# Two layers of a decoder on one core: fewer score pieces in the Top-64 stages, three probability buffers and an earlier turn of the maxima in the dense cross attention

## The chip, the core and the metric

One core of a Trainium2 chip runs the whole program. Its engines are TensorE (PE, matrix products into PSUM), VectorE (DVE), ScalarE (ACT), GpSimd (POOL) and SyncE (SP, which issues DMA transfers here). They run side by side, each through its own instruction list in order, and are held together by semaphores. The metric is the time of one execution on the device in microseconds (us).

## The reference, cut to what matters

Two decoder layers over 2,048 tokens of width 256 with a context of 1,601 tokens. The two stages with Top-64 have 16 heads of width 16:

```
# layer 0, cross attention: 2048 queries, 1601 keys, 16 heads
vals, idx = jax.lax.top_k(scores, 64)
scores = full_like(scores, neg).at[..., idx].set(vals)
ctx = softmax(scores) @ vh
# layer 1, self attention: 2048 queries, 2048 keys, 16 heads
top_scores, top_idx = jax.lax.top_k(scores, 64)
out = softmax(top_scores) @ gathered v
# layer 1, dense cross attention: 2048 queries, 1601 keys, 16 heads of width 64
attn = softmax(einsum('bqhd,bkhd->bhqk', q * SCALE, k))
out = einsum('bhqk,bkhd->bqhd', attn, v)
```

Around them stand a causal attention, a mixture of experts, a last linear layer and the norms.

## The kernel before

**Order of the stages.** `decoder` calls them one after the other, with a barrier between: load, `l0ac` (causal), `l0xc` (`attend_top`, 1,601 keys), experts, `l1ac` (`attend_top`, 2,048 keys), the wide projections, `l1xc` (`attend_wide`), `finish_wide`, the last linear layer. Within a stage each engine has a list of its own, written out by hand, and `hold` puts the semaphore waits before a step.

**`attend_top`.** A tile is 128 queries of one head against all keys, so a stage has 16 x 16 = 256 tiles. For tile n:
- PE forms the scores in 4 chunks (`search`, L557) into two PSUM banks, and ACT copies them to one of 4 score buffers (L652, tiles `l0xc_score` or `l1ac_score` and `keep_xT`). ACT may do so when `checked` and `masked` say that the tile four before is finished with the buffer.
- DVE cuts the row in `NSEG` = 64 pieces, all `nk // 64` wide but for the last. `MAX8` takes the 8 largest of each piece (L745) to `cand`, ordered so that the largest of all pieces come first, then the second largest, and so on.
- In the next tile's time DVE draws the 64 largest from `cand` in 8 rounds, each a `MAX8` (L764, `tops`) and, but for the last, a match-and-replace (L766). Round r reads only the first `UPTO[r]` candidates, `NSEG` times 1, 1, 1, 2, 2, 3, 4, 8. Between two steps of this chain stand pieces of the new tile (`some_segments`), so the chain's own waits are covered.
- ACT counts how many scores are above and below the 64th value found (`count`, L658 and L662), PE sums this over the queries (`flag`, L602) and ACT stores it (L667, `anyflag`). Late in the tile after the next DVE reads it (`check`, L780). If it isn't zero, DVE draws the 64 largest from the whole row again (L790 and L792, 15 steps) and writes the mask anew (L797, L799): the fallback. It counts up `checked` (L802).
- POOL writes the mask of the scores below the 64th value (L527). PE adds it to the transposed scores (`unit`, L571 and L573), ACT takes the exponential (`weigh`, L680), PE forms the weighted sums (L585), and after each chunk of 4 tiles it turns them (`combine`, L596).

**`attend_wide`.** For each head the keys stand in 13 tiles (`NKT`), 12 of 128 and one of 65. PE computes scores transposed, key by query, in key tile j (`by_key`: L1926 adds the shift by the row maximum, L1930 the product); ACT takes the exponential of 4 chunks of 512 queries to the probability buffer `prob[buf(j)]` (L2015); PE forms the sums of the key tile before (`sums`, L1942); POOL stages a value tile (L1888) and adds the probabilities of all key tiles to `total` (L1878, and L1875 for tiles 0 and 1 in one step), from which PE forms the denominators (L1952). `freed(h, j)` is the number of additions that ACT waits for before it writes the buffer of tile j.

Beside head `hb` runs the search for the row maxima of the next head `ha`: 64 jobs (16 query tiles, 4 key chunks), which `jobs_of(j)` spreads over the key tiles. A job is two matmuls on PE (`by_query`, L1915 and L1916) into one of 3 banks and a reduction on DVE (L2057). After the last of them DVE counts up `stats_set` (`a_set`), PE turns the 16 columns of maxima (`a_end`, L1987), DVE splits them in two parts (`a_split`), and SP sends them by 8 small DMAs (L1843) to the row `shift`, which PE needs for key tile 0 of the next head.

```
def buf(j):
    return 2 if j == NKT - 1 else j % 2
def freed(h, j):
    if j >= 2 and j < NKT - 1:
        return added_after(h, j - 2)
    return ADDS * (h - 1) + {0: NKT - 3, 1: NKT - 2, NKT - 1: NKT - 1}[j] + ADDS
```

## Time and profile before

| | us |
|---|---|
| median of 3 runs (9,355.04 to 9,376.61) | 9,370.65 |
| the profiled execution, own time | 9,320.69 |
| its span in the trace | 9,318.9 |
| DVE busy | 6,784.5 (73%) |
| PE busy | 6,964.9 (75%) |
| ACT busy | 4,490.9 (48%) |
| POOL busy | 3,923.4 (42%) |

The shares are means over stages with different limits, so each stage has to be read by itself: first the slices of the page, then the busy times of its stretch, then the order of the instructions in one tile. Busy times of overlapping instructions are counted once. A row of the timeline has the start, the time to the end of the last of its instructions, the engine, the line, the operation with its tiles and the count; in brackets stands the idle time before it and what ended it.

### The profile page before, as it was taken

Reading aid. Unit: us, or ns where it says so; the run is one execution under the profiler, and the core shown is the slowest. Engines: PE = TensorE matmul, PEld = TensorE weight load, DVE = VectorE, ACT = ScalarE, POOL = GpSimd, SP = SyncE. Lnnn points to the kernel's source line nnn. Section 1 sums busy time; section 2 is a strip of 40 time slices with the busy share of each in tenths; the row PEclk is TensorE's granted clock in tenths of the full one; section 3 lists DMA queues with packets and bytes.
Section 4 is the critical chain, followed back from the end, with each engine's and each line's share of the span. In section 5 each row is a group of like instructions: output and inputs, shape, how many; then the busy total and the mean of one; then the engine's idle time right before and its main releaser. Section 6 shows DMA issues by size and latency. Waiting matters only on the chain. (4 is left out here: it accounts for less than half of the span.)

```text
span 9318.9 us, 164285 instructions
## 1 busy us (share of the span) xinstructions
PE 6964.9 (75%) x31345; PEld 2804.8 (30%) x31468; DVE 6784.5 (73%) x47597; ACT 4490.9 (48%) x8515; POOL 3923.4 (42%) x2595
## 2 busy tenths in 40 slices
PE   6998667666666656999666666666656899999983
PEld 2333222222222224555222222222223322222212
DVE  2764599999999993554699999999997344344423
ACT  1564466666666652111476776677655322222220
POOL 0000255454545541221365656556553055555550
PEclk7998666666666665999666776766767999999986
DMA  2000000000000000000000000000000411111113
GB/s 62 26 21 5 34 5 8 5 8 5 8 6 7 8 1 16 14 20 10 35 5 8 5 8 5 8 5 8 5 5 9 161 30 29 29 40 32 29 30 73
DMA packets 81598, 193.31 MB, mean 21 GB/s; under 512 B 23728, under 2 KB 38062, under 8 KB 77230
## 3 DMA queue, kind: packets, MB, share of 16 engines
q1 hardware_dynamic: 72366, 169.98, 6.5%
q10 hardware_dynamic: 8192, 12.59, 0.5%
q14 instruction: 769, 6.30, 0.2%
q8 instruction: 271, 4.44, 0.2%
HBM read 118.97 MB, written 62.76 MB: 20 GB/s over the span
## 5 line engine op out<-in xcount | busy, mean ns | idle before, releaser
L2057 DVE TENSOR_REDUCE l1xc_part_max<-l1xc_by_query 128x1 f32<-128x512 f32 (+1 forms) x1024 | 558.0, 571 | 865.3 <-PE l1xc_by_query L1916 772.7
L557 PE MATMUL l1ac_by_query<-l1ac_k_stack,l1ac_q_stack 97*128 (+1 forms) x1024 | 441.5, 497 | 790.8 <-ACT keep_xT L652 436.3
L2015 ACT ACTIVATE l1xc_prob<-l1xc_less_max 128x512 f32<-128x512 f32 (+1 forms) x832 | 451.3, 594 | 1118.7 <-PE l1xc_less_max L1930 973.7
L745 DVE MAX8 l1ac_cand<-l1ac_score 128x8 f32<-128x32 f32 x8192 | 956.3, 185 | 27.9 <-ACT l1ac_score L652 16.9
L745 DVE MAX8 l1ac_cand<-keep_xT 128x8 f32<-128x32 f32 x8192 | 953.4, 183 | 4.4
L557 PE MATMUL l0xc_by_query<-l0xc_k_stack,l0xc_q_stack 97*128 (+2 forms) x1024 | 387.9, 448 | 724.2 <-ACT keep_xT L652 505.4
L745 DVE MAX8 l0xc_cand<-l0xc_score 128x8 f32<-128x25 f32 (+1 forms) x8192 | 896.0, 177 | 33.6 <-ACT l0xc_score L652 15.8
L745 DVE MAX8 l0xc_cand<-keep_xT 128x8 f32<-128x25 f32 (+1 forms) x8192 | 897.4, 177 | 4.4
L527 POOL TENSOR_SCALAR l1ac_lost<-l1ac_score,l1ac_tops 128x2048 bf16<-128x2048 f32 x128 | 695.8, 5436 | 472.8 <-DVE l1ac_tops L764 472.8
L1878 POOL TENSOR_TENSOR l1xc_total<-l1xc_total,l1xc_prob 128x2048 f32<-128x2048 f32 (+1 forms) x176 | 793.8, 4510 | 71.5 <-POOL l1xc_v_tile L1888 71.2
L527 POOL TENSOR_SCALAR l1ac_lost<-keep_xT,l1ac_tops 128x2048 bf16<-128x2048 f32 x128 | 696.1, 5438 | 271.6 <-DVE l1ac_tops L764 271.6
L527 POOL TENSOR_SCALAR l0xc_lost<-l0xc_score,l0xc_tops 128x1601 bf16<-128x1601 f32 x128 | 554.8, 4334 | 514.3 <-DVE l0xc_tops L764 509.2
L527 POOL TENSOR_SCALAR l0xc_lost<-keep_xT,l0xc_tops 128x1601 bf16<-128x1601 f32 x128 | 554.7, 4333 | 310.5 <-DVE l0xc_tops L764 310.5
L764 DVE MAX8 l1ac_tops<-l1ac_cand 128x8 f32<-128x64 f32 (+4 forms) x2048 | 669.6, 327 | 0.3
L764 DVE MAX8 l0xc_tops<-l0xc_cand 128x8 f32<-128x64 f32 (+4 forms) x2048 | 669.4, 327 | 0.4
L680 ACT ACTIVATE l1ac_prob<-l1ac_less_max 128x512 f32<-128x512 f32 x1024 | 583.5, 590 | 109.8 <-PE l1ac_less_max L573 103.0
L571 PE MATMUL l1ac_less_max<-l1ac_far,l1ac_lost 128*128 128x128 bf16 x4096 | 561.4, 282 | 4.2 <-POOL l1ac_lost L527 4.2
L680 ACT ACTIVATE l0xc_prob<-l0xc_less_max 128x512 f32<-128x512 f32 (+1 forms) x832 | 483.0, 592 | 154.7 <-PE l0xc_less_max L573 153.7
L573 PE MATMUL l1ac_less_max<-l1ac_q_stack,l1ac_k_stack 100*128 (+1 forms) x1024 | 550.4, 537 | 0.0
L571 PEld LDWEIGHTS l1ac_less_max<-l1ac_far,l1ac_lost 128*128 128x128 bf16 x4096 | 390.6, 129 | 528.2 <-issue 507.3
L1309 DVE TENSOR_REDUCE l0ac_part_max<-l0ac_by_query 128x1 f32<-128x512 f32 (+3 forms) x640 | 366.9, 608 | 196.3 <-PE l0ac_by_query L1173 85.9
L1930 PE MATMUL l1xc_less_max<-l1xc_q,l1xc_k 64*128 64x512 f32 (+1 forms) x1664 | 499.3, 678 | 0.0
(455 smaller groups left out, 14631.2 us busy)
## 6 DMA issues: line engine op xcount, KB each, us to landing
l1xc_k<-wide_k SPq DMA_DIRECT2D x32, 400.2 KB, 5.2
moe_w<-in_L_ffn_mlp_w_dram SPq DMA_DIRECT2D x16, 512.0 KB, 4.2
wide_q<-l1xp_full SPq DMA_DIRECT2D x8, 1024.0 KB, 3.9
wide_q_parts<-l1xp_parts SPq DMA_DIRECT2D x16, 512.0 KB, 5.3
l1xc_q_hm<-wide_q_parts SPq DMA_DIRECT2D x32, 256.0 KB, 3.8
l1xc_q<-wide_q SPq DMA_DIRECT2D x32, 256.0 KB, 5.7
wide_sums<-l1xc_o_out ACTq DMA_DIRECT2D x64, 128.0 KB, 2.3
l1xf_num<-wide_sums SPq DMA_DIRECT2D x16, 512.0 KB, 11.7
```

What stands on the lines that cost most here:

```text
L527: nc.gpsimd.tensor_scalar(lost[:, i % 8, 0:nk], score[i % 4][:, 0:nk], tops[:, i % 8, TOPK - 1:TOPK], None, ALU.is_lt).then_inc(masked, 1)
L557: nc.tensor.matmul(sA[c % 2][:, 0:w], Qm[0:SHIFT_ROW, bass.ds(at + i * P, P)], Kb[0:SHIFT_ROW, bass.ds(at + a, w)], start=True, stop=True) ...
L571: nc.tensor.matmul(bank[0:w, t * P:(t + 1) * P], lost[:, (4 * c + t) % 8, j * P:j * P + w], far[:], start=(t == 0), stop=False, skip_group ...
L573: nc.tensor.matmul(bank[0:w], Kb[:, bass.ds(at + j * P, w)], Qm[:, bass.ds(at + c * CH, CH)], start=False, stop=True, skip_group_check=Tru ...
L680: nc.scalar.activation(prob[0:w, k % 2, j % 4], yP[y_bank(c, j)][0:w], ACT.Exp).then_inc(y_taken, 1)
L745: seg = nc.vector.max(new[:, j:8 * NSEG:NSEG], score[i % 4][:, a:a + w])
L764: ins = nc.vector.max(some, part)
L1309: nc.vector.tensor_reduce(part_max[:, i % 2, c:c + 1], sA[k % 3][:, 0:seen_keys(i, c)], AX.X, ALU.max).then_inc(a_taken, 1)
L1878: nc.gpsimd.tensor_tensor(total[0:n], total[0:n], prob[0:n, buf(j)], ALU.add).then_inc(added_p, 1)
L1930: nc.tensor.matmul(yP[r][0:n], k32[half, key], q32[half, at], start=False, stop=True).then_inc(y_formed, 1)
L2015: nc.scalar.activation(prob[0:n, buf(j), c], yP[c % 2][0:n], ACT.Exp).then_inc(y_taken, 1)
L2057: nc.vector.tensor_reduce(part_max[:, i % 2, c:c + 1], a_bank(i, c)[:, 0:w], AX.X, ALU.max).then_inc(a_taken, 1)
```

## The change

It has two parts. In `attend_top` the row is cut in 52 pieces in place of 64. Their edges are rounded evenly, so the pieces have 30 or 31 columns with 1,601 keys and 39 or 40 with 2,048. `cand` and the prefixes `UPTO` follow `NSEG`. In `attend_wide` the probability and value buffers go round in three (tile 12 takes buffer 1), `freed` follows, the 64 jobs are spread over the first 11 key tiles (tiles 0 to 8 have 6, tiles 9 and 10 have 5; before, tiles 0 to 3 had 6 and tiles 4 to 11 had 5), and `a_set`, `a_end` and `a_split` stand one key tile earlier.

```
-    NSEG = 64
-    seg_w = nk // NSEG
-    segs = [(j * seg_w, seg_w if j < NSEG - 1 else nk - j * seg_w) for j in range(NSEG)]
+    NSEG = 52
+    edges = [(2 * j * nk + NSEG) // (2 * NSEG) for j in range(NSEG + 1)]
+    segs = [(edges[j], edges[j + 1] - edges[j]) for j in range(NSEG)]
...
-            return 2 if j == NKT - 1 else j % 2
+            return 1 if j == NKT - 1 else j % 3
...
-            early = len(jobs) - 5 * (NKT - 1)
+            early = len(jobs) - 5 * (NKT - 2)
             start = 5 * j + min(j, early)
-            return jobs[start:start + 5 + (1 if j < early else 0)] if j < NKT - 1 else []
+            return jobs[start:start + 5 + (1 if j < early else 0)] if j < NKT - 2 else []
...
-            if j >= 2 and j < NKT - 1:
-                return added_after(h, j - 2)
-            return ADDS * (h - 1) + {0: NKT - 3, 1: NKT - 2, NKT - 1: NKT - 1}[j] + ADDS
+            if j == NKT - 1:
+                return added_after(h, NKT - 3)
+            if j >= 3:
+                return added_after(h, j - 3)
+            return added_after(h - 1, (NKT - 4, NKT - 1, NKT - 2)[j])
...
-                    if j == NKT - 1 and ha is not None:
+                    if j == NKT - 2 and ha is not None:
                         a_end(ha)
...
+                    if j == NKT - 3 and ha is not None:
+                        a_set(ha)
                     if j == NKT - 2 and ha is not None:
-                        a_set(ha)
-                    if j == NKT - 1 and ha is not None:
                         a_split(ha)
```

DVE at the start of a tile of l0xc, before: pieces (`cand<-keep_xT`) between the steps of the chain.

```order
L764 MAX l0xc_tops<-l0xc_cand 128x8
L745 MAX l0xc_cand<-keep_xT 128x8 x4
L766 MATCH_REPLACE l0xc_cand<-l0xc_tops,l0xc_cand 128x64
L745 MAX l0xc_cand<-keep_xT 128x8 x4
L764 MAX l0xc_tops<-l0xc_cand 128x8
L745 MAX l0xc_cand<-keep_xT 128x8 x4
L766 MATCH_REPLACE l0xc_cand<-l0xc_tops,l0xc_cand 128x64
L745 MAX l0xc_cand<-keep_xT 128x8 x3
L764 MAX l0xc_tops<-l0xc_cand 128x8
L745 MAX l0xc_cand<-keep_xT 128x8 x4
```

The same place in the change:

```order
L764 MAX l0xc_tops<-l0xc_cand 128x8
L745 MAX l0xc_cand<-keep_xT 128x8 x3
L766 MATCH_REPLACE l0xc_cand<-l0xc_tops,l0xc_cand 128x52
L745 MAX l0xc_cand<-keep_xT 128x8 x3
L764 MAX l0xc_tops<-l0xc_cand 128x8
L745 MAX l0xc_cand<-keep_xT 128x8 x3
L766 MATCH_REPLACE l0xc_cand<-l0xc_tops,l0xc_cand 128x52
L745 MAX l0xc_cand<-keep_xT 128x8 x3
L764 MAX l0xc_tops<-l0xc_cand 128x8
L745 MAX l0xc_cand<-keep_xT 128x8 x3
```

Three pieces stand between the steps in place of 3 or 4, and the replaced prefix has 52 candidates in place of 64.

PE at the end of a head of l1xc, before (L1987 is the turn of the maxima, L1942 sums, L1926 and L1930 the scores of a key tile; 65 rows are key tile 12):

```order
L1915 MATMUL l1xc_by_query<-l1xc_k_hh,l1xc_q_hm 128x65
L1916 MATMUL l1xc_by_query<-l1xc_k_m,l1xc_q_hm 128x65
L1942 MATMUL l1xc_o_sum<-l1xc_prob,l1xc_v_tile 64x512 x2
L1987 MATMUL l1xc_den<-keep_ident,l1xc_stat 16x128
L1777 ISA
L1926 MATMUL l1xc_less_max<-l1xc_shift,l1xc_onesb 65x512 x2
L1930 MATMUL l1xc_less_max<-l1xc_q,l1xc_k 65x512 x2
L1942 MATMUL l1xc_o_sum<-l1xc_prob,l1xc_v_tile 64x512 x2
L1777 REGISTER_ALU
L1926 MATMUL l1xc_less_max<-l1xc_shift,l1xc_onesb 65x512 x2
L1930 MATMUL l1xc_less_max<-l1xc_q,l1xc_k 65x512 x2
L1942 MATMUL l1xc_o_sum<-l1xc_prob,l1xc_v_tile 64x512 x2
```

The same place in the change, where the lines are two further down:

```order
L1944 MATMUL l1xc_o_sum<-l1xc_prob,l1xc_v_tile 64x512 x2
L1989 MATMUL l1xc_den<-keep_ident,l1xc_stat 16x128
L1777 ISA
L1928 MATMUL l1xc_less_max<-l1xc_shift,l1xc_onesb 128x512 x2
L1932 MATMUL l1xc_less_max<-l1xc_q,l1xc_k 128x512 x2
L1944 MATMUL l1xc_o_sum<-l1xc_prob,l1xc_v_tile 64x512 x2
L1777 REGISTER_ALU
L1928 MATMUL l1xc_less_max<-l1xc_shift,l1xc_onesb 128x512 x2
L1932 MATMUL l1xc_less_max<-l1xc_q,l1xc_k 128x512 x2
L1944 MATMUL l1xc_o_sum<-l1xc_prob,l1xc_v_tile 64x512 x2
L1777 ISA
L1928 MATMUL l1xc_less_max<-l1xc_shift,l1xc_onesb 65x512 x2
```

The turn now stands before key tile 11 (128 rows), and key tiles 11 and 12 follow it without jobs of the search.

## Rows read from the trace of the kernel before

**Rows 1.** The page, busy tenths of DVE in 40 slices of the span.

```profile
...
DVE  2764599999999993554699999999997344344423
...
```

**Rows 2.** Busy time in three stretches (l0xc, l1ac, l1xc); columns in the first line.

```profile
...
core 0: us, PE busy (x) PEld busy (x) DVE busy (x) ACT busy (x) POOL busy (x), PEclk, DMA share, GB/s
1060.00:3520.00 2460.00, 1638.20 (x7782) 644.81 (x7783) 2424.36 (x21958) 1488.61 (x3038) 1221.55 (x882) 0.61 0.02 6
4540.00:7110.00 2570.00, 1702.78 (x9093) 687.19 (x9092) 2547.79 (x21950) 1755.06 (x3217) 1502.22 (x883) 0.69 0.02 6
7400.00:9061.00 1661.00, 1510.60 (x6245) 395.45 (x6352) 655.07 (x1327) 469.98 (x865) 914.64 (x398) 0.94 0.14 31
...
```

**Rows 3.** Timeline of DVE in an l0xc tile (start, us, instructions), and a page row.

```profile
...
2042.86 0.67 DVE L764 MAX8 l0xc_tops<-l0xc_cand 128x8 f32<-128x512 f32 x1
2043.45 0.77 DVE L745 MAX8 l0xc_cand<-keep_xT 128x8 f32<-128x25 f32 x8
...
L745 DVE MAX8 l0xc_cand<-l0xc_score 128x8 f32<-128x25 f32 (+1 forms) x8192 | 896.0, 177 | 33.6 <-ACT l0xc_score L652 15.8
...
```

**Rows 4.** Timeline of DVE, first and next instruction of the fallback in l0xc and l1ac.

```profile
...
3350.72 1.83 DVE L790 MAX8 l0xc_top_full<-keep_xT 128x8 f32<-128x1601 f32 x1
...
3382.62 0.09 DVE L766 MATCH_VALUE_LOAD l0xc_cand<-l0xc_tops,l0xc_cand 128x8 f32 x1 [0.61 <-DVE l0xc_lost L799]
...
6782.69 2.28 DVE L790 MAX8 l1ac_top_full<-l1ac_score 128x8 f32<-128x2048 f32 x1
...
6821.97 0.09 DVE L766 MATCH_VALUE_LOAD l1ac_cand<-l1ac_tops,l1ac_cand 128x8 f32 x1 [0.33 <-DVE l1ac_lost L799]
...
```

**Rows 5.** Waits in the l0xc stretch: total us, times, longest.

```profile
...
ACT keep_xT L652 <- DVEq L802: 441.8, 126, 33.7
...
```

**Rows 6.** Timeline of ACT in l0xc, and two loads of the flag (line 780).

```profile
...
2023.30 1.09 ACT L652 ACTIVATE keep_xT<-l0xc_by_query 128x512 f32<-128x512 f32 x2 [3.41 <-DVEq L802]
...
2033.34 1.08 ACT L652 ACTIVATE l0xc_score<-l0xc_by_query 128x512 f32<-128x512 f32 x2
...
2038.82 0.16 ACT L667 ACTIVATE l0xc_anyflag<-l0xc_turned 1x1 f32<-1x1 f32 x1
...
L780 DVEq TENSOR_LOAD <-l0xc_anyflag x1: 305/305/305, 2022.6 to 2022.6; - x1
...
L780 DVEq TENSOR_LOAD <-l0xc_anyflag x1: 304/304/304, 2041.4 to 2041.4; - x1
...
```

**Rows 7.** Waits in the l1xc stretch: total us, times, longest.

```profile
...
ACT l1xc_prob L2015 <- POOL l1xc_total L1875: 103.6, 16, 6.6
...
```

**Rows 8.** Timeline of PE in one head of l1xc, rows of line 1926.

```profile
...
7853.32 0.39 PE L1926 MATMUL l1xc_less_max<-l1xc_shift,l1xc_onesb 2*128 2x512 bf16 x2 [3.35 <-DMA l1xc_shift<-l1xc_stat_parts]
...
7858.81 0.39 PE L1926 MATMUL l1xc_less_max<-l1xc_shift,l1xc_onesb 2*128 2x512 bf16 x2
...
7863.33 0.39 PE L1926 MATMUL l1xc_less_max<-l1xc_shift,l1xc_onesb 2*128 2x512 bf16 x2
...
7866.86 0.39 PE L1926 MATMUL l1xc_less_max<-l1xc_shift,l1xc_onesb 2*128 2x512 bf16 x2
...
7870.38 0.39 PE L1926 MATMUL l1xc_less_max<-l1xc_shift,l1xc_onesb 2*128 2x512 bf16 x2
...
7877.14 0.39 PE L1926 MATMUL l1xc_less_max<-l1xc_shift,l1xc_onesb 2*128 2x512 bf16 x2 [2.76 <-ACT l1xc_prob L2015]
...
7882.25 0.39 PE L1926 MATMUL l1xc_less_max<-l1xc_shift,l1xc_onesb 2*128 2x512 bf16 x2
...
7944.44 0.40 PE L1926 MATMUL l1xc_less_max<-l1xc_shift,l1xc_onesb 2*65 2x512 bf16 x2
...
7952.83 0.40 PE L1926 MATMUL l1xc_less_max<-l1xc_shift,l1xc_onesb 2*128 2x512 bf16 x2 [3.40 <-DMA l1xc_shift<-l1xc_stat_parts]
...
```

**Rows 9.** Busy time and granted clock of short stretches of l1xc, columns as rows 2.

```profile
...
7952.90:7956.40 3.50, 3.17 (x8) 0.97 (x10) 0.04 (x1) 1.08 (x2) 1.99 (x1) 0.53 0.56 135
...
8052.70:8072.00 19.30, 19.08 (x51) 4.07 (x54) 3.84 (x7) 4.31 (x8) 2.29 (x2) 0.50 0.58 130
...
```

## The prediction

> **What bounds the kernel now.** I read the page's slices first, then the busy times of three stretches, then the order of instructions inside one tile of each. [rows 1] VectorE (DVE) shows 9s in two long blocks, slices 6 to 15 and 21 to 30. They are the two Top-64 stages, l0xc (1,601 keys) and l1ac (2,048 keys). [rows 2] In them DVE is busy 2,424 of 2,460 us and 2,548 of 2,570 us, while TensorE (PE) has about two thirds and ScalarE (ACT) 60 to 68%. So DVE sets their time, and every nanosecond that it drops is worth one, until a neighbour becomes late. The third row of [rows 2] is the dense cross attention l1xc: PE 1,511 of 1,661 us, nothing else above 914. It is bound by PE, and a gain there is either idle time of PE or a higher clock.
>
> [rows 6] One l0xc tile per 9.40 us: the two value loads stand two tiles apart, 2022.6 and 2041.4. A tile has 64 `MAX8` over pieces (25 columns) and a chain of 8 `MAX8` and 7 match-and-replace over the candidates.
>
> **Part 1, fewer pieces.** What a `MAX8` costs DVE is the distance to the next start, not its duration, since they overlap: eight pieces take 0.77 us from the first start to the last end, one lasts 0.177, so the other seven are (0.77 - 0.177)/7 = 0.085 us apart [rows 3]. The one over 512 candidates blocks for 2043.45 - 2042.86 = 0.59 us. Two points give a line: 0.085 = f + 25s, 0.59 = f + 512s, so s = 1.04 ns a column and f = 59 ns an instruction. The columns of a row stay (1,601 or 2,048), so 12 pieces less save 12 x 59 = 0.71 us a tile. The chain reads 1+1+1+2+2+3+4+8 = 22 piece counts in its `MAX8` and 14 in its replacements: 36 x 12 = 432 columns less, 0.45 us. Together 1.16 us a tile: 9.40 to 8.24 in l0xc, and in l1ac, with 447 columns more, 9.87 to 8.71. For 2 x 256 tiles: **-594 us**. Between two chain steps now 3 pieces stand in place of 3 or 4, some 0.27 us against 0.21 us for the shortest step with its own 0.13 already behind it, so the chain's waits stay covered.
>
> Priced by duration (0.177 us for 25 columns, so some 0.15 fixed) the 12 pieces would be worth 1.8 us a tile. The Trainium skill says something near that ("VectorE: DVE Perf Modes", section on the TRN2 errata): its table has 58 cycles fixed, but it finds about 150 measured for a single operation and calls this an overhead that many small tiles pay each time. By the 150 the 12 pieces save 1.9 us; by the trace's distances 0.7. Two neighbours overlap here, so I keep 0.7.
>
> **What the wider pieces bring back.** Each piece gives only its 8 largest. If 9 of a row's 64 lie in one piece (or the short prefixes of the first rounds take a wrong value) the count misses, and `check` does the whole row again. This is a matter of the data, so I worked it out from the reference: its scores for the drawn inputs, in float32, cut both ways. With 64 pieces no row of l0xc fails and one of l1ac (head 14, tile 0); with 52 pieces 4 rows of l0xc in 4 tiles and 4 of l1ac in 4 tiles, each with 9 in one piece. The trace has one fallback in each stage [rows 4], so l0xc has one that the cut does not explain; I take it for two equal scores at the cut, which comes again. So 4 more in l0xc and 3 more in l1ac. [rows 4] One costs 3382.62 - 3350.72 = 31.9 us in l0xc and 6821.97 - 6782.69 = 39.3 in l1ac, and DVE does nothing else: 4 x 31.9 + 3 x 39.3 = **+246 us**. PE, ACT and GpSimd (POOL) only drain meanwhile.
>
> **Who is late next.** DVE waits for ACT at two places: the scores of the next tile, and the flag before `check`. [rows 5] ACT itself waits 441.8 us in 126 turns for `checked` on one pair of score buffers, so it has slack of 2 to 3 us a tile that shrinks by 1.16. The scores come most of a tile early. The flag is nearer. [rows 6] The ACT slot that ends a chunk (every fourth) runs from 2023.30 to 2033.34, 10.04 us, longer than a tile already; the next begins 1.3 us after a check (2022.6 + 9.4) and its flag is out 5.6 us later, at 2038.98, 2.4 us before the load at 2041.4. With 8.24 us a tile the slow slot starts 0.7 us after its check and ends 10.74 - 8.24 = 2.5 us after the next one; 2.5 + 5.6 is 8.1 us against 8.24, and a slot that is 0.6 us slower in its matmuls (an estimate) makes it 8.7. DVE then waits up to 0.5 us at 64 such places: 0 to 32 us. I take **+30**, since the granted clock there is 0.61 in the mean, nearer to half than to full [rows 2]. l1ac has 0.47 us more in each tile for the same slot, and I take none. POOL's mask keeps below a tile in both.
>
> **Part 2, the dense cross attention.** Three things move.
> (a) *Three probability buffers.* Before, key tile 2 shared its buffer with tile 0, and the first addition (4.5 us on POOL) reads 0 and 1 together. ACT waits for it in each of 16 heads, 103.6 us [rows 7]. On PE the tile takes 7882.25 - 7870.38 = 11.87 us against 7.05 for tile 1, with as many matmuls [rows 8]: 2.76 us idle, the rest slower matmuls behind it. After, tile 2 has its own buffer and tile 3 finds the addition done. Tile 12 now takes buffer 1, and the next head's tile 1 waits for its addition, which ends some 5 us into tile 0; it is needed after about 8. Gain 4.8 us a head.
> (b) *Maxima turned at the last but one key tile.* The transpose stands right before 7944.44, the shifts land at 7952.83, and PE is idle 3.40 us at the head's border [rows 8]. A tile earlier the same 8.6 us lie under two tiles without scores, about 10.3 us. Gain 3.4 us. SP's queue is not held up: its K and Q loads follow these DMAs and are for the next head.
> (c) *The score jobs* of tile 11 go to tiles 4 to 8, one more each. The same matmuls, so nothing in sum; DVE takes six reductions in a tile elsewhere already. Without them POOL (5.2 us a tile) is close behind PE for two tiles; 0 to 0.5 us a head.
> *The clock.* After such an idle stretch PE runs at half: granted clock 0.53 from 7952.90 [rows 9], the 1.2 GHz level. That doubles the first part of key tile 0: 7858.81 - 7853.32 = 5.49 us against 3.53 at tile 1 [rows 8], 1.96 us more. Together (a), (b) and the clock are 10.2 us for each of 15 borders, 152; behind some borders the half clock lasts longer (0.50 over 19.3 us, second row), which I price at 20 for all of them. Lower end: only the idle time, 2.8 + 3.4 in 15 heads, 93. Upper end 180. I take **-165**, near the upper end, since rows show the clock lost right behind the idle stretch. The Trainium skill agrees in kind ("TensorE: Matmul & The Clock Gate", "Why this matters for your kernels"): idle gaps between bursts of matmuls bring the half rate back.
>
> **The sum.** -594 + 246 + 30 - 165 = -483 us against the profiled run's own 9,320.7 us (span 9,318.9). The median of the shown runs is 50 us higher, 9,370.65; the difference carries over: **8,888 us**.
>
> **The rivals.**
> - *The wait for the flag takes the place of the pieces.* If ACT and PE cannot follow, DVE idles before `check` and about half of part 1 stays away. For it: the 10.04 us slot. Against it: that slot is one in four and ACT idles behind the others. +297: 9,185.
> - *The wait in l1xc only moves.* Additions on POOL or the DMA of the shifts become late at another tile, and the clock keeps falling. Only some 30 of 165 us come: 9,023.
> - *Slower: the fallbacks multiply.* The chip's scores are sums of split parts, not my float32. Without fallbacks the change is worth 594 - 30 + 165 = 729 us, and one costs 35.6 on average: above 20 more fallbacks it loses. With 30 more, 9,710. Against it: a miss is decided by which piece a score stands in, and my rows with 9 are decided far above rounding; the cut before gave the counts that the trace has, but for one.
> - *Pieces priced by duration.* If a piece frees its whole fixed 0.15 us, part 1 gives 600 us more: 8,290. Against it are the distances in [rows 3]. The rule of the Trainium skill above would make this time.
> - *It does not do what it says*: the fallbacks stay at two, since the misses of 52 pieces do not occur on the chip: 8,888 - 246 = 8,642.
>
> **How the numbers follow.** My case 0.74, flag 0.08, moved wait in l1xc 0.10, slower 0.03, priced by duration 0.02, no more fallbacks 0.03. Own range of my case: two fallbacks fewer or two more (72), the flag 0 to 60, l1xc -93 to -180, runs that differ by 20: 8,800 to 8,990. To hold 8 in 10 it takes in the near side of the moved wait: 8,800 to 9,010. A measurement of this kernel can tell about 0.2% (19 us) from no change. All cases but one are faster by more: faster 0.96, same 0.01, slower 0.03.
>
> **What would show it.** In the profile after: value loads 8.24 and 8.71 us apart, with 52 pieces between; long `MAX8` rows (1,601 columns) in 5 tiles and (2,048) in 4; DVE still in the 9s of both blocks. An idle time of DVE before the load of the flag would speak for the first rival. In l1xc: no wait of ACT for POOL at key tile 2, no wait of PE for the shift DMA, key tiles 0 and 2 near 8.1 and 7.1 us, a granted clock near 1.0 throughout, the stretch near 1,495 us. I am wrong if the number of fallbacks is not near nine, or if the tiles do not shorten by the fixed cost of 12 pieces.

## The result, and the profile after

| | before | after |
|---|---|---|
| median, us (4 runs each, on one chip) | 9,362.85 | 8,966.16 |
| lowest to highest | 9,352.21 to 9,376.61 | 8,950.63 to 8,971.08 |
| the profiled execution, own time | 9,320.69 | 8,971.08 |

The ratio is 0.9583, with a 95% interval from 0.9558 to 0.9607: the change takes 397 us off, where 483 were forecast (8,888, range 8,800 to 9,010). The sign, the two waits that went and the number of fallbacks came as predicted. 86 us of the gain stayed away, about half in each part of the change; a new wait of PE for ACT, which the prediction did not have, and idle time of DVE that it put too low are behind most of it.

The busy times of the three stretches in the profile after, columns in the first line; they answer to [rows 2]:

```profile
core 0: us, PE busy (x) PEld busy (x) DVE busy (x) ACT busy (x) POOL busy (x), PEclk, DMA share, GB/s
1060.00:3400.00 2340.00, 1538.75 (x7784) 615.84 (x7785) 2266.07 (x19009) 1471.44 (x3041) 1224.99 (x883) 0.65 0.02 6
4420.00:6840.00 2420.00, 1620.57 (x9069) 657.88 (x9068) 2371.56 (x18952) 1741.65 (x3218) 1499.19 (x882) 0.72 0.02 6
7165.00:8712.00 1547.00, 1469.45 (x6350) 383.46 (x6348) 659.39 (x1328) 469.95 (x865) 914.37 (x398) 0.98 0.15 34
```

DVE still fills the two Top-64 stages, with about 3,000 instructions fewer in each, but it now stands idle for 74 us in l0xc and 48 in l1ac, against 36 and 22 in [rows 2]. PE's granted clock in l1xc rose from 0.94 to 0.98.

The same chain steps as in [rows 3] and the order rows of the change, DVE in l0xc after:

```profile
2054.38 0.30 DVE L764 MAX8 l0xc_tops<-l0xc_cand 128x8 f32<-128x156 f32 x1
2054.60 0.36 DVE L745 MAX8 l0xc_cand<-l0xc_score 128x8 f32<-128x31 f32 x3
2054.88 0.07 DVE L766 MATCH_VALUE_LOAD l0xc_cand<-l0xc_tops,l0xc_cand 128x8 f32 x1
```

Three pieces of 31 columns take 2054.88 - 2054.60 = 0.28 us from start to start, 0.093 each, and 156 candidates take 2054.60 - 2054.38 = 0.22. The line of the prediction gives 0.091 and 0.221.

The fallback's `MAX8` over a whole row (line 790, eight in each fallback) after; [rows 4] had one fallback a stage:

```profile
L790 DVE MAX8 l1ac_top_full<-l1ac_score x32: 2294/2295/2295, 4765.4 to 6653.8; 128x8 f32<-128x2048 f32 x32
L790 DVE MAX8 l0xc_top_full<-l0xc_score x24: 1827/1828/1830, 1126.4 to 2241.7; 128x8 f32<-128x1601 f32 x24
L790 DVE MAX8 l0xc_top_full<-keep_xT x16: 1828/1828/1830, 2297.4 to 3270.8; 128x8 f32<-128x1601 f32 x16
```

(24 + 16)/8 = 5 fallbacks in l0xc and 32/8 = 4 in l1ac, the nine that were forecast.

By stage, from the first to the last instruction in the two traces:

| us | before | after | difference |
|---|---|---|---|
| l0xc | 2,515.3 | 2,388.1 | -127.2 |
| l1ac | 2,626.7 | 2,479.5 | -147.2 |
| l1xc | 1,671.5 | 1,556.8 | -114.7 |
| all others | 2,505.4 | 2,544.9 | +39.5 |

The three stages give -389, 8 us short of what the medians show. Of the 39 us outside them 25.6 lie in l1af, the 16 output rows behind l1ac, whose code is the same. The profiled execution of before was 42 us quicker than its median, and its short l1af may be one reason; that is not shown. Two windows of 10 us at the same place in that stage, one of the run with attend_wide alone changed (l1af 36.0 us, as before) and one of after (61.6 us):

```profile
7129.00:7139.00 10.00, 10.00 (x44) 6.09 (x44) 2.46 (x6) 1.19 (x2) 0.00 (x0) 1.00 0.01 2
```

```profile
6890.00:6900.00 10.00, 10.00 (x23) 5.56 (x23) 1.27 (x3) 0.60 (x1) 0.00 (x0) 0.50 0.00 0
```

PE is busy throughout in both, with 44 matmuls at a granted clock of 1.00 (2.4 GHz) and 23 at 0.50 (1.2 GHz). Over all profiles of this study the stage took 36.0, 40.4 or 61.6 us, so a difference of 26 us there says nothing of a change.

### The profile page after: what moved, and what is told of

Its sections match the earlier page's. It is cut to its first block and busy times, and to the rows that moved or that the text cites. A ratio compares the mean times of both kernels' runs of the same rounds, so it can differ in the third digit from the quotient of the medians.

```text
span 8969.3 us, 158459 instructions
## 1 busy us (share of the span) xinstructions
PE 6782.5 (76%) x31468; PEld 2754.4 (31%) x31468; DVE 6449.7 (72%) x41621; ACT 4457.7 (50%) x8515; POOL 3925.8 (44%) x2595
## 5 line engine op out<-in xcount | busy, mean ns | idle before, releaser
L745 DVE MAX8 l1ac_cand<-l1ac_score 128x8 f32<-128x39 f32 (+1 forms) x6656 | 863.8, 193 | 28.7 <-ACT l1ac_score L652 16.8
L745 DVE MAX8 l1ac_cand<-keep_xT 128x8 f32<-128x39 f32 (+1 forms) x6656 | 863.7, 192 | 4.4
L745 DVE MAX8 l0xc_cand<-l0xc_score 128x8 f32<-128x31 f32 (+1 forms) x6656 | 801.9, 183 | 28.0 <-ACT l0xc_score L652 15.7
L745 DVE MAX8 l0xc_cand<-keep_xT 128x8 f32<-128x31 f32 (+1 forms) x6656 | 802.3, 182 | 4.4
L764 DVE MAX8 l1ac_tops<-l1ac_cand 128x8 f32<-128x52 f32 (+4 forms) x2048 | 598.6, 292 | 0.3
L764 DVE MAX8 l0xc_tops<-l0xc_cand 128x8 f32<-128x52 f32 (+4 forms) x2048 | 597.7, 292 | 0.3
L571 PE MATMUL l1ac_less_max<-l1ac_far,l1ac_lost 128*128 128x128 bf16 x4096 | 532.2, 270 | 7.7 <-POOL l1ac_lost L527 4.5
L573 PE MATMUL l1ac_less_max<-l1ac_q_stack,l1ac_k_stack 100*128 (+1 forms) x1024 | 527.0, 515 | 0.0
L571 PEld LDWEIGHTS l1ac_less_max<-l1ac_far,l1ac_lost 128*128 128x128 bf16 x4096 | 366.8, 122 | 491.4 <-issue 422.1
L1932 PE MATMUL l1xc_less_max<-l1xc_q,l1xc_k 64*128 64x512 f32 (+1 forms) x1664 | 474.7, 647 | 0.0
```

Source lines behind the costliest of these rows:

```text
L571: nc.tensor.matmul(bank[0:w, t * P:(t + 1) * P], lost[:, (4 * c + t) % 8, j * P:j * P + w], far[:], start=(t == 0), stop=False, skip_group ...
L573: nc.tensor.matmul(bank[0:w], Kb[:, bass.ds(at + j * P, w)], Qm[:, bass.ds(at + c * CH, CH)], start=False, stop=True, skip_group_check=Tru ...
L745: seg = nc.vector.max(new[:, j:8 * NSEG:NSEG], score[i % 4][:, a:a + w])
L764: ins = nc.vector.max(some, part)
L1932: nc.tensor.matmul(yP[r][0:n], k32[half, key], q32[half, at], start=False, stop=True).then_inc(y_formed, 1)
```

## The experiments

All were timed in five rounds beside the kernel before, in groups of four on one chip: e1 to e4, then e5, e6, e7 and e9, then e8, e11, e12 and e13 (before: 9,352, 9,364 and 9,346 us). A difference of medians between two groups carries the difference of these three numbers; the stages in the traces do not.

| run | median us | ratio to before, 95% interval |
|---|---|---|
| the change | 8,966 | 0.9583 [0.9558, 0.9607] |
| e1 pieces only | 9,092 | 0.9733 [0.9700, 0.9766] |
| e2 attend_wide only | 9,221 | 0.9875 [0.9842, 0.9908] |
| e3 three buffers only | 9,306 | 0.9961 [0.9941, 0.9981] |
| e4 earlier turn only | 9,275 | 0.9910 [0.9876, 0.9943] |
| e5 change, no second search | 8,616 | 0.9205 [0.9177, 0.9234] |
| e6 change, store spread | 8,906 | 0.9510 [0.9481, 0.9539] |
| e7 change, 51 and 53 pieces | 8,780 | 0.9366 [0.9336, 0.9396] |
| e8 e6 and e7 | 8,726 | 0.9330 [0.9297, 0.9364] |
| e9 change, combine late | 8,936 | 0.9534 [0.9504, 0.9564] |
| e11 e9 and flag early | 8,901 | 0.9520 [0.9483, 0.9556] |
| e12 e6, e7 and e11 | 8,685 | 0.9286 [0.9259, 0.9313] |
| e13 40 pieces, no second search | 8,419 | 0.9004 [0.8970, 0.9038] |

### The parts apart

e1 is the change with attend_wide as before.

> The change's part in attend_top alone (52 pieces with even edges), attend_wide as before. The prediction's terms give -594 for shorter tiles, +246 for 7 more fallbacks and +30 for the flag wait: -318 against before. The two traces (before and the whole change) show -127 in l0xc and -147 in l1ac: -274, with 8.30 us for a tile of l0xc and 8.72 of l1ac, 5 and 4 tiles of over 30 us, and the flag wait in one tile of four of l0xc. If what the trace shows is the parts' own and they don't touch each other: -274, near 9,089 us. If the stretch after l1ac (finish_rows, 36 to 62 us) belongs to this part, -249. A rival: some of the gain seen in the stages came from the heads of attend_wide through the clock; then less than 240 of it is here.

e2 is the kernel before with the changed attend_wide.

> The change's part in attend_wide alone, attend_top as before. The prediction had -165 for it; the traces show the PE stretch of l1xc going from 1,660.4 to 1,546.0, -114. Parts that add up: near 9,249 us (-114), and the sum of this run's and e1_pieces_only's differences is within 15 us of the whole change's -397. A rival: the stretch of l1xc has luck of the clock in it (two heads of the profiled run had 20 us at half clock); then this run's l1xc is nearer 1,500 and the time -150.

Measured: 0.9733 and 0.9875. The two gains add up, 0.0267 + 0.0125 = 0.0392 against 0.0417 of the whole change, within the intervals. In the traces e1's l0xc and l1ac are 2,388.3 and 2,478.3 us long, the whole change's to about 1 us, with 5 and 4 fallbacks; e2's l1xc is 1,550.5. So the parts don't touch each other, and each is worth less than its forecast: by the medians 260 us (318 forecast) and 132 (165). l1af was 61.6 us in e1 and 36.0 in e2.

### Two edits inside attend_wide

e3 has the buffers alone:

```
-            return 2 if j == NKT - 1 else j % 2
+            return 1 if j == NKT - 1 else j % 3
...
+            if j >= 3:
+                return added_after(h, j - 3)
```

> Before, with only the three buffers in turn (buf and freed) in attend_wide; the jobs and the turn of the maxima stay where they were. The wait of ACT for POOL at key tile 2 (103.6 us over 16) goes: key tile 2 of a head from 11.87 to 7.4, 15 times 4.45 = -67. Theory A, from the trace of the whole change: ACT's 8 DMA issues of store then lie in front of the exponentials of key tile 3, which becomes 1.5 us longer: +24; the wait for the shift row stays (3.4 a head, at times more). Sum -43, near 9,320. Rival B: the new wait at key tile 3 comes from the sixth job there and from the earlier turn, not from the store; then no wait is at key tile 3 here and the gain is -67 (9,296).

e4 has the jobs, `a_end`, `a_set` and `a_split` alone:

```
-            early = len(jobs) - 5 * (NKT - 1)
+            early = len(jobs) - 5 * (NKT - 2)
...
-                    if j == NKT - 1 and ha is not None:
+                    if j == NKT - 2 and ha is not None:
                         a_end(ha)
```

> Before, with only the earlier turn in attend_wide (64 jobs over 11 key tiles, a_set, a_end and a_split one key tile earlier); the buffers stay as they were. The wait for the shift row ahead of key tile 0 goes: 15 times 3.4 = -51, and the half clock behind it (about 2 us a head): -80 at most, near 9,285 to 9,312. Key tile 2 keeps its wait of 4.5 us for POOL, and since ACT is held there the store's issues cost nothing at key tile 3. With e3_buffers_only it should add up to e2_wide_only. Rival: the two idle times stand in for each other (PE's idle 4.5 us at key tile 2 throws the clock to half again, whatever comes at key tile 0); then this part alone gives under 40.

Measured: -46 us and -77 us (ratios 0.9961 and 0.9910), together -123 against -132 for both. Waits in the l1xc stretch. Before, beside the wait for POOL of [rows 7], ACT had this one (total us, times, longest):

```profile
ACT l1xc_prob L2015 <- issue: 41.3, 9, 5.0
```

Of e3:

```profile
ACT l1xc_prob L2017 <- issue: 73.3, 15, 5.6
PE l1xc_less_max L1928 <- DMA l1xc_shift<-l1xc_stat_parts: 57.4, 16, 7.8
```

and of e4:

```profile
ACT l1xc_prob L2015 <- POOL l1xc_total L1875: 103.7, 16, 6.6
PE l1xc_less_max L1926 <- DMA l1xc_shift<-l1xc_stat_parts: 7.8, 1, 7.8
```

Each edit removes the wait that it is aimed at and leaves the other one. e3 has lost the wait for POOL of [rows 7], but its ACT now stands 73.3 us at 15 places for "issue", that is for nothing that another engine owes it, where before had 41.3 at 9. Key tile 2 went from 11.85 to 7.45 us in e3 and key tile 3 from 7.56 to 8.72 (medians over heads 1 to 14 of 0 to 15), and PE stands 24.2 us for ACT inside tile 3 in place of 6.4. Theory A holds: the wait came with the buffers alone, without the earlier turn. e4 has the shift DMA only once, at the first head.

### What stands ahead of key tile 3

Where the 67.3 us of "issue" of the whole change lie, ACT in one head after (ACTq is ACT's queue, which issues a DMA):

```profile
7701.40 0.59 ACT L2017 ACTIVATE l1xc_prob<-l1xc_less_max 128x512 f32<-128x512 f32 x1
7701.94 0.81 ACTq L2034 DMA_DIRECT2D wide_sums<-l1xc_o_out  x1
7702.91 0.48 ACTq L2032 DMA_DIRECT2D wide_sums<-l1xc_o_out  x1
...
7706.10 0.48 ACTq L2034 DMA_DIRECT2D wide_sums<-l1xc_o_out  x1
7706.85 1.09 ACT L2017 ACTIVATE l1xc_prob<-l1xc_less_max 128x512 f32<-128x512 f32 x2 [4.85 <-issue]
```

and PE in the same head, line 1928 being the first matmul of a group:

```profile
7702.96 0.39 PE L1928 MATMUL l1xc_less_max<-l1xc_shift,l1xc_onesb 2*128 2x512 bf16 x2
7707.99 0.39 PE L1928 MATMUL l1xc_less_max<-l1xc_shift,l1xc_onesb 2*128 2x512 bf16 x2 [1.44 <-ACT l1xc_prob L2017]
7713.10 0.39 PE L1928 MATMUL l1xc_less_max<-l1xc_shift,l1xc_onesb 2*128 2x512 bf16 x2
```

Six of the eight issues of `store` stand from 7702.91 to 7706.10 at (7706.10 - 7702.91)/5 = 0.64 us each, and ACT's exponentials are behind them. PE waits 1.44 us for the bank. The tile then takes 7713.10 - 7702.96 = 10.14 us in place of 7.05: beside the idle time, PE's matmuls are slow for a while. Busy times and granted clock of that piece:

```profile
7709.50:7712.90 3.40, 3.40 (x8) 0.59 (x6) 1.39 (x2) 1.05 (x2) 0.00 (x0) 0.51 0.00 0
```

The clock 0.51 is the lower level, 1.2 GHz. It fell in this way behind the wait in three of the 15 heads that have it (3, 5 and 9, idle times of 1.44 to 2.00 us) and not in the others, though two of them stood longer (2.49 us in head 1, 2.19 in head 11). In the other heads that search for maxima the tile takes 8.2 to 9.6 us, and the idle time is nearly all of its excess.

e6 issues two after each of the key tiles 2 to 5:

```
-                    if j == 2 and not first:
-                        store(hb - 1)
+                    if 2 <= j < 2 + QC and not first:
+                        store(hb - 1, j - 2)
...
-                for c in range(QC):
+                for c in range(QC) if one is None else [one]:
```

> The changed kernel with the 8 DMA issues of store on ACT's queue spread out in attend_wide: two after each of the key tiles 2, 3, 4 and 5 in place of all eight after key tile 2. Theory A: these issues (about 0.64 us each, 5.1 in a row) delay the exponentials of key tile 3, and PE waits 24 us for them in sum and runs at half clock behind some of the waits; in the trace of the wide part alone key tile 3 is 8.2 to 11.0 us in place of 7.05, 29 us over 15 heads. Spread, 1.3 us stand between two key tiles, where ACT has over 4 us to spare: key tile 3 at 7.1, near 8,966 - 29 = 8,937 us. Rival B: the wait at key tile 3 is that for POOL, in a new place; then it stays and the time is 8,966. Rival C: the issues wait for the inverted denominators (DVE, key tile 1), which come late; then key tile 3 stays above 8.

Measured: 8,906 us, 60 less than the change. PE in the same head of e6, key tile 3 and the next:

```profile
7668.72 0.39 PE L1928 MATMUL l1xc_less_max<-l1xc_shift,l1xc_onesb 2*128 2x512 bf16 x2
7672.24 0.39 PE L1928 MATMUL l1xc_less_max<-l1xc_shift,l1xc_onesb 2*128 2x512 bf16 x2
7675.77 0.39 PE L1928 MATMUL l1xc_less_max<-l1xc_shift,l1xc_onesb 2*128 2x512 bf16 x2
```

The tile takes 7675.77 - 7668.72 = 7.05 us, and no head has a longer one. The stretch of l1xc in e6:

```profile
7137.00:8641.00 1504.00, 1452.77 (x6352) 381.92 (x6352) 657.66 (x1328) 469.93 (x865) 914.82 (x398) 0.99 0.15 35
```

PE's idle time fell from 75.4 to 50.6 us. ACT has no wait for "issue" left. l1xc as a stage is 42 us shorter. The excess of key tile 3 makes up 29 of them, as expected; most of the rest is that no head of this execution had the long stretch at half clock that two heads of after had (key tile 0 of 14.3 us against 8.4, and 9.0 against 7.05 for tile 1: 8 us a head). e5, which has this attend_wide unchanged and had no such head either, took 1,545.7 us against 1,514.6, so 31 us are the store's. A further 21 us of the 60 are l1af again (40.4 us).

### The price of the fallbacks

e5 reads the flag and never takes the branch; the second search is left out:

```
-                with dve.If(found > 0):
+                with dve.If(found > 2130706432):
```

> The changed kernel, in which DVE still reads the flag but never draws the 64 largest from the whole row again; left out is that second search, so that the 9 tiles with too many large scores in one piece keep a mask that is off. The trace of the change has 5 such tiles in l0xc with 159.2 us over the usual tile and 4 in l1ac with 157.4. If they stand on the path one for one, as the prediction has it: 8,966 - 316 = 8,650 us. A rival: behind a fallback the other engines are ahead, so that the next tiles run without the flag wait and give part back; then the price is under 300 and the time over 8,666. Another: the 5.6 us of half clock and the loop's ends hang on the fallbacks' places (they shift nothing in the program, but the phase of the clock); then single stages outside the two move by 20 us or more.

Measured: l0xc 2,388.1 to 2,229.1 and l1ac 2,479.5 to 2,322.1, which is -159.0 and -157.4, within 0.2 us the time that the nine had over the usual tile. So a fallback stands on the path one for one, and no tile behind it gives anything back. The median is 8,616, 350 less. The other 34 us are not explained; the profiled execution, 40 us quicker than the median, has l0af at 40.7 us in place of 62.0 and l1af at 36.0 in place of 61.6, which are stages that the edit does not touch.

e7 changes the count of pieces:

```
-    NSEG = 52
+    NSEG = 51 if tag == "l0xc" else 53
```

> The changed kernel with 51 pieces in l0xc and 53 in l1ac, edges rounded evenly as well. The number of pieces moves two things: 12 to 13 us for each piece fewer and stage (0.097 us a tile: 0.059 for the instruction and 36 columns at 1.04 ns), and where the edges fall, which decides by the data alone in which tiles a piece holds more than 8 of the 64. Counted from the scores, the redone tiles are 2 in l0xc (in place of 5) and 2 in l1ac (in place of 4). Theory: l0xc -96 -25 = -121, l1ac -79 +25 = -54, sum -175: 8,791 us. Rival: the flag wait takes more of l0xc's tile (0.1 us in one tile of four, 6 us, or in all of them, 25); then 8,797 to 8,816. If the count of redone tiles has nothing to do with the edges, the time stays within 15 us of 8,966.

Measured: 8,780 us. Line 790 in e7:

```profile
L790 DVE MAX8 l0xc_top_full<-l0xc_score x8: 1828/1828/1828, 2166.5 to 2193.0; 128x8 f32<-128x1601 f32 x8
L790 DVE MAX8 l0xc_top_full<-keep_xT x8: 1828/1828/1828, 3133.2 to 3159.7; 128x8 f32<-128x1601 f32 x8
L790 DVE MAX8 l1ac_top_full<-keep_xT x8: 2295/2295/2295, 5345.3 to 5378.3; 128x8 f32<-128x2048 f32 x8
L790 DVE MAX8 l1ac_top_full<-l1ac_score x8: 2294/2295/2295, 5580.1 to 5613.1; 128x8 f32<-128x2048 f32 x8
```

Two fallbacks in each stage, as counted from the scores. One of l0xc, in head 14, query tile 14, is in before, in the change and in e7 alike: it is the one that the cut did not explain. It came again, as the prediction took it to; that two equal scores are its reason was not tested. l0xc is 111 us shorter and l1ac 60 (121 and 54 expected); in l0xc the wait for the flag takes 8 us more. One piece more or less moved a stage by 60 to 110 us, mainly through the edges: the number of pieces itself is worth 25 us a stage. This holds for these inputs only: with others the edges fall elsewhere.

### The wait for the flag

Idle time of DVE in l0xc before a value load of the chain (line 766). It is where DVE stands when `check` has waited for the flag; the profile calls it "issue". After:

```profile
DVE l0xc_cand L766 <- issue: 46.9, 98, 3.4
```

And before:

```profile
DVE l0xc_cand L766 <- issue: 11.5, 58, 0.6
```

The longer tile is every fourth one: 41 of the 60 that are neither a fallback nor at an end of the loop over heads are over 8.69 us from value load to value load, most of them 8.8, against 8.29. ACT at such a place after: the end of the slot that ends a chunk of four tiles, the next tile's scores, and the flag:

```profile
1865.41 0.23 ACT L690 ACTIVATE l0x_o_all<-l0xc_turned 128x68 f32 x1 [1.67 <-PE l0xc_turned L596]
...
1866.66 1.08 ACT L652 ACTIVATE l0xc_score<-l0xc_by_query 128x512 f32<-128x512 f32 x2
...
1872.75 0.16 ACT L667 ACTIVATE l0xc_anyflag<-l0xc_turned 1x1 f32<-1x1 f32 x1 [0.78 <-PE l0xc_turned L602]
```

and DVE behind it:

```profile
1873.06 0.18 DVE L745 MAX8 l0xc_cand<-keep_xT 128x8 f32<-128x31 f32 x1
1874.01 0.09 DVE L766 MATCH_VALUE_LOAD l0xc_cand<-l0xc_tops,l0xc_cand 128x8 f32 x1 [0.77 <-issue]
```

ACT stands 1.67 us for PE's `combine`, its copies of the scores start at 1866.66, the flag is out at 1872.91, 6.25 us later, and DVE has 0.77 us of idle time where the other tiles have 0.27. That is the wait that the prediction put at 0 to 0.5 us. Its way of adding it up holds too: scores 2.42 us behind the check (2.5 forecast), the flag 6.25 us later (5.6, and 0.6 for slower matmuls) and 0.13 to the load give 8.80.

e9 moves `combine` and `take_combined` to the next slot:

```
+                if exists(*before_it) and quad_before(*before_it)[2] == 3:
+                    combine(ho, co, h * QT + i - SET if settles(*before_it) else H * QT)
                 if exists(h, i):
                     sums(hq, cq, kq)
...
-                if ending:
-                    combine(hq, cq, h * QT + i - SET + 1 if settles(h, i) else H * QT)
```

> The changed kernel with combine (PE) and take_combined (ACT) of a chunk moved from the end of the fourth slot to the next slot, behind its scores and ACT's count. Theory of the flag wait: in one tile of four of l0xc ACT's copies of the next scores come late, since ACT stands 1.7 us for PE's combine; DVE then waits 0.46 to 0.50 us more for the flag. Without that stand the longer tiles (23 us in l0xc, 4 in l1ac) are gone: near 8,939 us, all tiles of l0xc at 8.30. Rival: the longer tile comes from DVE's own list (its positions in the ring of 4 buffers), or combine, put in the next slot, delays the flag there as much; then the same excess shows in another tile of the four and the time stays at 8,966, or rises by up to 20.

Measured: 8,936 us, 30 under the change, but in the trace l0xc is only 3.5 us shorter and l1ac 1.8, so the stages don't bear out a gain of 30. The scores are now 0.68 us behind the check, in place of 2.42, but the flag comes 7.8 us after them in place of 6.25. The longer tiles have 0.30 us in place of 0.50. Both sides of the expectation were half right: the stand delayed the scores, and the new place of `combine` delayed the flag nearly as much.

e11 puts the flag right behind `combine`, ahead of the sums:

```
                     combine(ho, co, h * QT + i - SET if settles(*before_it) else H * QT)
+                    if settles(h, i):
+                        flag(h * QT + i - SET, (i - SET) % QT, 4 * hq + cq if exists(h, i) else 0)
```

> The kernel with combine and take_combined in the next slot (8,936 us), in which PE now forms the flag right behind combine and ahead of the sums and the third unit. There the scores of the next tile were on time (0.67 us after the check in place of 2.42), but the flag came 7.8 us after them in place of 6.25, behind combine and the sums, so that the longer tile only fell from 0.50 to 0.30 us. Theory: with the flag ahead of the sums it comes about 2 us earlier, no tile of l0xc waits for it, and the excess of the tiles 3, 7 and 11 of each head goes to under 0.1: l0xc near 2,365 against 2,388 and 2,385. Rival: PE then stands for ACT's take_combined before the flag (the flag needs it), and the sums and the weights behind it come late; then ACT's next scores are late, and the excess is in the tile after.

Measured: 8,901 us. DVE in the l0xc stretch of e11:

```profile
DVE l0xc_cand L777 <- issue: 19.2, 65, 0.8
```

The excess of the tiles 3, 7 and 11 of a head is 0.01 us, and the flag is out 2.07 us before its load there, where it was 0.13 (medians). l0xc is 30.6 us shorter than in the change and l1ac 13.0: more than the 23 and 4 us of the longer tiles, since the idle time at the ends of the loop over heads went down too (from 21.2 to 11.7 us in l0xc). PE does stand 0.51 us for `take_combined` in front of the flag, as the rival said, but the tile behind is not longer. The median is 65 us under the change; the two stages account for 44, and l1af, at 36.0 in place of 61.6, for 26.

e13 asks how far this goes, with 40 pieces and without the second search:

```
-    NSEG = 52
+    NSEG = 40
```

> The changed kernel with 40 pieces in place of 52 and without the second search; left out is the redoing of the tiles with more than 8 large scores in one piece, so that those tiles keep a mask that is off. It asks where the flag's way round takes over from DVE. By DVE's own work a tile would be another 1.16 us shorter: 7.14 us in l0xc and 7.55 in l1ac, 594 us under the run without the second search (8,616): 8,022. The way round, read from the trace of the change (check to the next scores 0.67, scores to flag 5.0, 5.4, 6.5 and 6.25, flag to check 0.13, and 1.75 more in the fourth for combine), is 5.8, 6.2, 7.3 and 8.8 us in l0xc and 6.3, 7.0, 7.8 and 8.9 in l1ac. Theory: a tile takes the longer of the two, so that one in four stays at 8.8, and the means are 7.6 and 8.0: near 8,250 us. Rival: the way round is not what holds a tile (the score buffers or ACT's own work of some 6 us are); then all four kinds of tile are longer by the same, or all are at 7.14.

Measured: 8,419 us. Of the 594 us by which DVE's own work should shrink against e5, 198 came. Waits in the l0xc stretch of e13:

```profile
DVE l0xc_cand L766 <- issue: 156.7, 95, 5.3
DVE l0xc_cand L766 <- ACT l0xc_anyflag L667: 74.9, 56, 2.4
ACT keep_xT L652 <- POOL l0xc_lost L527: 152.6, 63, 3.2
```

DVE idles 232 us where the change had 47. In l0xc, of four tiles one stands at DVE's own 7.31 us, one at 7.33 or 7.65, one at 7.95 to 8.4 and one at 9.1 to 9.9; the mean is 8.2 in l0xc and 8.4 in l1ac. In the last two kinds DVE reads the flag 0.13 us after it is out, so the way round by the flag holds these and not the others, as the theory said. But the sum was 170 us too low. Three things in the trace point the same way; none of them was varied alone. The mask on POOL, which ACT must await before it overwrites the buffer, now comes late at 63 places (third row). The copies of the scores behind the chunk's end start 3.36 us after the check, not 2.42, since less of ACT's stand is hidden. And DVE's own tile is 7.31 us and not 7.14: 12 pieces fewer were worth 0.98 us this time, not 1.16.

### Together

e8 has the edits of e6 and e7, e12 those of e11 as well.

> The changed kernel with 51 pieces in l0xc and 53 in l1ac, and with the store's DMA issues spread over key tiles 2 to 5. The two were run alone: 8,780 and 8,906 us, 186 and 60 under the change's 8,966. They lie in different stages, so they should add up: near 8,725 us with the stages' own differences (-175 and -43 in the traces give 8,748; the medians give 8,720). If they don't add, the time is over 8,765.

> All three together: 51 and 53 pieces, the store spread, combine in the next slot with the flag right behind it. If each keeps its worth: 8,725 less 25 to 30 (the flag wait of l0xc and l1ac): near 8,698 us. If the earlier flag brings nothing, 8,725.

Measured: 8,726 and 8,685 us. By the medians the gains of e6 and e7 add up within 6 us (by the ratios e8 is 0.0037 short of their sum, 35 us, where its own interval reaches 0.0034 to either side); in e8's trace l0xc, l1ac and l1xc are within 2.4 us of those of e7 and e6. The flag edits bring 41 us more in the same group. e12 has ratio 0.9286 to before and is 281 us below the change, so it beats both kernels; its number of pieces is fitted to these inputs.

## Right and wrong, point by point

- **Which engine bounds which stage: right.** DVE in l0xc and l1ac, PE in l1xc; e1 and e2 add up.
- **Part 1, -594 us: nearly.** The line through two distances of [rows 3] forecast 8.24 and 8.71 us a tile; the traces have 8.29 and 8.70 to 8.72. That is 1.11 and 1.15 us a tile, over 255 distances each -576. The rival that priced a piece by its duration is dead. (Its sum was also too large: with the fixed 0.15 us from the rows the 12 pieces give 560 us more, not 600.) With it falls, for this kernel, the reading of the Trainium skill that priced it ("VectorE: DVE Perf Modes", section on the TRN2 errata): some 150 cycles fixed for each of many small instructions is not what these traces show, as neighbours without a dependence start 0.092 us apart at a duration of 0.182. The same section's table, 58 cycles and one for each column, is an estimate of 0.093 us for 31 columns at its 0.96 GHz, and it fits the distances though not the durations.
- **Fallbacks, +246: right to 1 us.** 5 and 4 of them, 31.8 and 39.3 us over the usual tile each: four more in l0xc and three in l1ac came to 245, and e5 shows that they stand on the path whole.
- **The flag, +30: the place right, the sum too low.** In l0xc the fourth tiles grew by 20 us, mostly 0.5 us each: that is what I had counted, and it lies in my 0 to 32. But I counted only those. Over all tiles but the fallbacks DVE's excess over the usual tile rose from 29.7 to 57.8 us in l0xc and from 15.6 to 42.2 in l1ac, +55 where I had 30. The fourth tiles of l1ac grew by 12 us where I took none, the ends of the loop over heads by 4 us in l0xc and 10 in l1ac, and single tiles elsewhere, 0.3 us each, by 5 in each stage. e11 shortens the two stages by 44 us with the order of `combine` and the flag alone; the 0.3 us tiles stay, and their cause is open. The term that was mis-sized is this one, and the step is "I take none" for l1ac, with no term for the loop's ends.
- **Part 2 (a), 4.8 us a head: the wait went, and a new one came.** "Tile 3 finds the addition done" was true of POOL and overlooked ACT's own list: eight DMA issues stand between the exponentials of tiles 2 and 3. Before, they cost little because PE itself was late at tile 2, behind the wait of [rows 7] (key tile 3 had 7.56 us in place of 7.05). This term is the largest miss in l1xc: e6 takes it away and the stretch is 1,503 us, against 1,495 forecast (of the 43 us between the two kernels 12 to 16 are the two heads with the long half clock, which no run ties to the edit: luck, as far as is known). A smaller slip: tile 2 has as many matmuls as tile 1, but one long job in place of a short one, so it fell to 7.45 and not to 7.05, 4.4 us and not 4.8.
- **Part 2 (b), 3.4 us a head: the DMA wait went, but not all of the idle time.** PE's idle time before key tile 0 fell from 57.5 to 20.8 us over the heads. 7.7 of these are the first head's, and 11.3 stand as "issue" at the six ends of the loop over pairs of heads, where key tile 12 is 6.6 to 7.1 us long in place of 5.14. That is not the shift; that it lay under the wait for it before is my reading, as no run varied the loop. Key tile 0 itself is 8.42 us in most heads, 10.0 in two and 14.3 in two, where 8.1 was forecast.
- **The clock: in kind right.** Half clock behind an idle stretch went with the stretch (0.94 to 0.98 to 0.99 in e6): between the first key tile of the first head and the last of the last, PE had the lower level for 191 us before, 51 after and 14 in e6. Behind the new waits in key tile 3 it came in three heads of 15. So "a granted clock near 1.0 throughout" was nearly right. The direction agrees with the Trainium skill ("TensorE: Matmul & The Clock Gate", "Why this matters for your kernels"), that idle gaps bring the half rate back.
- **The rivals.** "The wait for the flag takes the place" was real in kind but not at 52 pieces; e13 shows it at 40, where two thirds of the gain stay away. "The wait in l1xc only moves" was right for one of the two waits, at a third of its price. The slower ones did not come.

The sum of the prediction with measured terms: -576 + 245 + 55 = -276 for part 1 and -115 for part 2, -391, beside -397 in the medians. The two misses have the same sign and did not cancel: 8,966 is 78 us above the 8,888, near the upper end (8,990) of the range of my own case. The range held; the idle time of the Top-64 stages and the store's issues are why it was needed.

## What to carry to other kernels

When a wait goes, read on in the list of the engine that was waiting: what stood behind the wait for free (here eight DMA issues of 0.64 us on ACT) is next on the path. Here spreading them cost nothing that the trace shows. When an engine's own work shrinks, follow the round trips that it takes part in once for every kind of tile, not for the mean: one tile in four with a longer slot decided. And where an approximation has an exact fallback, count the fallbacks from the data for each setting before choosing it, as one of 39 us outweighs the gain of one piece less.

## What the runs showed of the hardware

- A DMA issue on ACT's queue takes 0.64 us of ACT's time from one to the next, eight of them 5.1 us. The Trainium skill ("DMA: Bandwidth & Descriptors", "Issuing engines are not separate DMA queues") says that spreading issues over engines saves only the issue time, usually small beside the transfer; here that time was what PE waited for.
- The same code ran at either clock level in different executions: l1af 36.0, 40.4 or 61.6 us, l0af 40.6 or 62.0, l0xf 50.4 to 61.6. In l1xc of before the first key tile of a head took 15.6 us in four heads, and in e1, with the same code there, in seven: 18 us more for the stretch. I found no cause in the rows. Differences under some 30 us of a whole run should be read from the stage, not from the total.
- `MAX8` on DVE: start to start 0.092 us for 31 columns, 0.101 for 40, 0.114 for 52, 0.276 for 208 and 0.493 for 416, all on the line of 59 ns and 1.04 ns a column, as long as other instructions stand between a result and its use. In the fallback, where the next instruction needs the result, 1,601 columns take 1.863 us from start to start, over the duration of 1.828; the line would give 1.724.
